# Context attention: weighing by split bf16 products, the maxima's split by ScalarE and GpSimd, and the terms' low halves by GpSimd

## The reference, cut to what matters

```python
# stage 4 (and stage 6 without mask, 8 heads): query 4x512, context 4x154
scores = jnp.einsum('bhqd,bhkd->bhqk', q, k)
scores = jnp.where(mask[:, None, :, :], -1e18, scores)
attn = jax.nn.softmax(scores, axis=-1)
context = jnp.einsum('bhqk,bhkd->bhqd', attn, v)
```

## Time and profile before

| | |
|---|---|
| median of three runs | 1929.69 us (1927.9 to 1934.78) |
| profiled execution, its own time | 1934.83 us |
| its span | 1933.0 us |
| PE busy / DVE / ACT / POOL over the span | 78% / 62% / 41% / 39% |
| mean granted TensorE clock | 0.868 of full speed |
| stage 4, units of the context attention | about 1103 to 1271 us of the span |
| stage 6, units of the context attention | about 1496 to 1607 us of the span |

### The profile page before, as it was taken

The page is one execution under the profiler, slowest core; times in us unless marked ns, Lnnn a source line. Parts: engine busy times, 40 slices in busy tenths (PEclk is TensorE's granted clock), DMA queues, the critical chain, the costliest instruction groups (busy, mean ns, idle before and its releaser), DMA issues.

```text
span 1933.0 us, 32091 instructions
## 1 busy us (share of the span) xinstructions
PE 1515.4 (78%) x11458; PEld 990.6 (51%) x11581; DVE 1205.2 (62%) x2958; ACT 802.1 (41%) x1806; POOL 757.9 (39%) x909
## 2 busy tenths in 40 slices
PE   4899989979998986574268789958976886478877
PEld 2677757766776665452155345523443333334544
DVE  5777667767766655547947657644465465676653
ACT  3677557747765644320035245533212452211111
POOL 3788668858755863510012342000002101143320
PEclk9999989999998997776558799989985697779887
DMA  6223211211211102400000000000000000000000
GB/s 243 76 87 106 76 52 42 55 35 41 53 38 42 51 20 84 150 20 1 0 1 1 11 4 2 1 1 1 1 1 1 1 1 1 1 1 6 1 6 12
DMA packets 35443, 63.94 MB, mean 33 GB/s; under 512 B 7527, under 2 KB 25026, under 8 KB 34131
## 3 DMA queue, kind: packets, MB, share of 16 engines
q1 hardware_dynamic: 33815, 59.77, 10.3%
q0 software_dynamic: 1472, 2.12, 0.3%
HBM read 30.59 MB, written 12.66 MB: 22 GB/s over the span
## 4 chain that ended last, share of the span: by engine, by line
PE 62%; DVE 24%; POOL 5%; issue 5%; ACT 3%; DMA 1%; SPq 0%; DVEq 0%; ACTq 0%; POOLq 0%
PE banks L475 14%; PE banks L694 8%; PE banks L709 6%; PE banks L683 6%; PE banks L1876 4%; DVE xn L421 3%; PE banks L1859 2%; PE banks L450 2%; POOL work L963 2%; PE banks L1785 1%; DVE norm_room L405 1%; PE banks L1826 1%; DVE work L744 1%; PE banks L2565 1%; PE banks L1516 1%
## 5 line engine op out<-in xcount | busy, mean ns | idle before, releaser
L963 POOL TENSOR_TENSOR work<-work 128x512 bf16<-128x512 f32 (+1 forms) x448 | 373.2, 863 | 47.6 <-ACT work L852 44.4
L837 ACT ACTIVATE work<-banks,work 128x666 f32<-128x666 f32 x256 | 209.2, 817 | 198.7 <-DVE work L744 163.3
L415 POOL TENSOR_TENSOR norm_room<-norm_room,minus_half 128x4 f32<-128x4 f32 x48 | 50.2, 1046 | 537.7 <-DVE norm_room L410 537.6
L744 DVE TENSOR_REDUCE work<-banks 128x1 f32<-128x666 f32 x256 | 216.1, 844 | 60.6 <-PE banks L683 60.1
L694 PE MATMUL banks<-const,work 128*128 128x128 f32 (+1 forms) x1536 | 218.5, 279 | 30.0 <-ACT work L852 25.8
L758 DVE COPY work<-banks 128x256 f32<-128x256 f32 x256 | 106.7, 417 | 123.7 <-PE banks L694 123.5
L694 PEld LDWEIGHTS banks<-const,work 128*128 128x128 f32 (+1 forms) x1536 | 156.5, 135 | 51.9 <-ACT work L837 29.3
L683 PE MATMUL banks<-work 128*128 128x154 bf16 (+1 forms) x932 | 172.2, 304 | 7.8 <-DMA work<-work 2.6
L475 PE MATMUL banks<-work,weights_b 128*128 128x512 bf16 (+1 forms) x830 | 157.2, 347 | 12.8 <-DVE work L2200 5.5
L709 PE MATMUL banks<-work 128*64 128x256 bf16 x2304 | 160.7, 284 | 7.5 <-POOL work L963 6.3
L852 ACT ACTIVATE work<-banks 128x512 f32<-128x512 f32 x256 | 151.3, 591 | 10.1 <-PE banks L694 9.8
(11 more groups left out here) (398 smaller groups left out, 3059.7 us busy)
## 6 DMA issues: line engine op xcount, KB each, us to landing
work<-work SPq DMA_DIRECT2D x128, 166.5 KB, 3.0
sorted<-in_pads SPq DMA_DIRECT2D x10, 838.5 KB
weights_b<-in_weights SPq DMA_DIRECT2D x1, 4120.0 KB, 23.4
work<-scratch SPq DMA_DIRECT2D x64, 64.0 KB, 2.0
weights_b<-in_weights SPq DMA_DIRECT2D x1, 2824.0 KB, 9.6
weights_a<-in_weights SPq DMA_DIRECT2D x1, 2056.0 KB, 8.1
weights_a<-in_weights SPq DMA_DIRECT2D x1, 2050.0 KB, 9.4
work<-work SPq DMA_DIRECT2D x32, 64.0 KB, 1.9
```

Of the source, the lines that this page charges most:

```text
L744: ve.tensor_reduce(self.neg_max[i % 4], self.slot[i % 2][:, 0:KEYS0], AX_X, ALU.max, negate=True).then_inc(self.mark("max"))
L837: ac.activation(self.probs[i % 3], self.slot[i % 2][:, 0:KEYS0], ACT.Exp, bias=self.neg_max[i % 4], accum_out=self.sums[u % 4][:, 2 * j + ...
L963: po.tensor_tensor(parts[:, :, :, 0], exact, parts[:, :, :, 1], ALU.subtract).then_inc(self.mark(event, i - 3))
```

## The change

The weighing is done in bf16: with values v and terms t both split as high + low, the product v.t becomes high.high + high.low + low.high (the pairs (1,1), (1,0) and (0,1) of the code, 1 being the upper half; low.low is left out), and the sums need two products, since the ones are exact. So a weighing has 12 + 8 bf16 products of 256 columns in place of 4 + 4 float32 ones. What it needs in addition are the low halves: of the values, once a batch by POOL (`values_low`), and of every term, by POOL, except for two of the 20 a unit in stage 4, which DVE does (`low_by_ve`). The split of the maxima goes from DVE to ACT (high part) and POOL (low part). A chunk is weighed two chunks behind the terms and no longer one, and the last chunk after the "lift" of the next unit; the ring of term tiles grows from 12 to 16. POOL now walks through the sorted list as the others do, so that masks, heads and `query_low` get due times. The rest chunk's mask product in stage 4 is taken over all 128 rows (rows without keys are zeroed once) and no longer over 26.

```diff
-HALF, TERMS = SEQ // 2, 12
+HALF, TERMS = SEQ // 2, 16
...
                 terms += [("term", u, c, g) for g in range(GROUPS)]
-                if c:
-                    terms.append(("weigh", u, c - 1, 0))
-            terms.append(("weigh", u, a.chunks - 1, 0))
+                if c >= 2:
+                    terms.append(("weigh", u, c - 2, 0))
+            terms.append(("weigh", u, a.chunks - 2, 0))
             out += [(u + 1.38 + 0.88 * i / len(terms), *item) for i, item in enumerate(terms)]
-            out += [(u + 2.27 + 0.1 * j, "divide", u, j, 0) for j in range(2)]
-            out.append((u + 2.56, "finish", u, 0, 0))
+            out += [(u + 1.44 + 0.88 * i / len(terms), "low", *item[1:]) for i, item in enumerate(terms) if item[0] == "term"]
+            out.append((u + 2.33, "weigh", u, a.chunks - 1, 0))
+            out += [(u + 2.36 + 0.1 * j, "divide", u, j, 0) for j in range(2)]
+            out.append((u + 2.6, "finish", u, 0, 0))
+        for b in range(1, BATCH):
+            out += [(2 * b - 1.6, "mask", b, 0, 0), (2 * b - 0.8, "query_low", b, 0, 0), (2 * b + 0.3, "mask_t", b, 0, 0)]
+            out += [(2 * b - 1.5 + 0.12 * g, "heads", b, g, 0) for g in range(GROUPS + 1)]
...
+    def low_by_ve(self, a, c, g):
+
+        return a.stage == 4 and c % 2 == 1 and g == 0
...
                 if s == 4:
-                    mask = a.mask_t[b % 2]
-                    if c < a.per_group:
-                        m = pe.matmul(bank, self.cb["eye_b"], mask[:, 0, cols], start=False, stop=True)
-                    else:
-                        m = pe.matmul(bank, self.cb["four_eyes"][0:CTX_REST, :], mask[0:CTX_REST, 1, cols], start=False, stop=True)
+                    mask, rest = a.mask_t[b % 2], c == a.per_group
+                    m = pe.matmul(bank, self.cb["four_eyes" if rest else "eye_b"], mask[:, int(rest), cols], start=False, stop=True)
...
-                pe.wait_ge(*self.at("exp4", s, n))
-                for of_sums in (0, 1):
+                pe.wait_ge(*self.at("term_low", s, n))
+                if self.low_by_ve(a, c, 0):
+                    pe.wait_ge(*self.at("term_low_0", s, n - GROUPS + 1))
+                terms = [self.halves(self.term(a, u, c, g)[3]) for g in range(GROUPS)]
+                values = [self.halves(a.values[b % 2][0:rows_n, c, g, :]) for g in range(GROUPS)]
+                for of_values, of_terms in ((1, 1), (1, 0), (0, 1)):
                     for g in range(GROUPS):
-                        left = a.block[0:rows_n, c, :] if of_sums else a.values[b % 2][0:rows_n, c, g, :]
-                        m = pe.matmul(self.bank_of(5)[WIDE * g:WIDE * (g + 1), of_sums * HALF:(of_sums + 1) * HALF], left,
-                                      self.term(a, u, c, g)[3], start=c == 0 and not of_sums, stop=c == a.chunks - 1, skip_group_check=True)
+                        pe.matmul(self.bank_of(5)[WIDE * g:WIDE * (g + 1), 0:HALF], values[g][:, :, of_values], terms[g][:, :, of_terms],
+                                  start=c == 0 and of_values == of_terms == 1, stop=False, skip_group_check=True)
+                for of_terms in (1, 0):
+                    for g in range(GROUPS):
+                        m = pe.matmul(self.bank_of(5)[WIDE * g:WIDE * (g + 1), HALF:SEQ], self.halves(a.block[0:rows_n, c, :])[:, :, 1],
+                                      terms[g][:, :, of_terms], start=False, stop=c == a.chunks - 1, skip_group_check=True)
...
+            elif what == "negate":
+                ac.wait_ge(*self.at("most", s, 2 * a.steps * (u + 1) - 1))
+                ac.wait_ge(*(self.at("lifted", s, u - 2) if u >= 2 else self.at("clear_shift", s)))
+                ac.activation(a.shift[u % 2][:, :, 0, 0:a.heads], a.most[u % 2], ACT.Copy).then_inc(self.mark("shift_high", s, u))
...
+            for mask in a.mask_t:
+                i = po.memset(mask[:, 1, :], 0.0)
+            po.wait_ge(*self.own("po", i))
             self.mask_t_po(po, a, 0)
-            self.follow_power(po, 3, BATCH - 1)
-        for b in range(1, BATCH):
-            if s == 4:
-                self.mask_po(po, b)
-            self.heads_of(po, a, b)
-            self.query_low(po, a, b)
...
+        for what, u, c, g in self.context_items(a):
+            if what == "negate":
+                out = a.shift[u % 2][:, :, :, 0:a.heads]
+                po.wait_ge(*self.at("shift_high", s, u))
+                po.tensor_tensor(out[:, :, 1, :], a.most[u % 2], out[:, :, 0, :], ALU.subtract).then_inc(self.mark("shift", s, u))
+            elif what == "low" and not self.low_by_ve(a, c, g):
+                n, _, _, whole = self.term(a, u, c, g)
+                po.wait_ge(*self.at("exp4", s, n))
+                po.tensor_tensor(self.halves(whole)[:, :, 0], whole, self.halves(whole)[:, :, 1],
+                                 ALU.subtract).then_inc(self.mark("term_low", s, n))
+            elif what == "values":
+                po.wait_ge(*self.at("values", s, u))
+                for rows, chunks in ((P, slice(0, a.per_group)), (a.rest, slice(a.per_group, a.chunks))):
+                    whole = a.values[u % 2][0:rows, chunks, :, :].rearrange("p c g n -> p (c g n)")
+                    i = po.tensor_tensor(self.halves(whole)[:, :, 0], whole, self.halves(whole)[:, :, 1], ALU.subtract)
+                i.then_inc(self.mark("values_low", s, u))
```

More of the change, by code:

```diff
@@ L1964, in context_ve @@
                                  a.block[0:a.rest, a.per_group:a.chunks, :].to_broadcast([a.rest, GROUPS, WIDE]), ALU.mult).then_inc(self.mark("values", s, u))
[L1965 to L1970 removed]
+            elif what == "low" and self.low_by_ve(a, c, g):
+                n, _, _, whole = self.term(a, u, c, g)
+                ve.wait_ge(*self.at("exp4", s, n))
+                ve.tensor_tensor(self.halves(whole)[:, :, 0], whole, self.halves(whole)[:, :, 1],
+                                 ALU.subtract).then_inc(self.mark("term_low_0", s, n))
             elif what == "divide":
@@ L1984, in context_ve, with heads_of @@
                 self.follow_scale(ve, u, c)
-    def heads_of(self, po, a, b):
-        last = 2 * a.chunks * GROUPS
-        if b >= 3:
-            po.wait_ge(*self.at("termed", a.stage, (b - 2) * last - 1))
-        for g in range(GROUPS):
+    def heads_of(self, po, a, b, g):
+        if b >= 3 and g == 0:
+            po.wait_ge(*self.at("termed", a.stage, (b - 2) * 2 * a.chunks * GROUPS - 1))
+        if g < GROUPS:
             if b in (0, 2):
```

35 lines of the change are left out of this document (19 added, 16 removed).

## The result

The changed kernel takes 1953.07 us (median, 1949.47 to 1955.14) where the kernel before takes 1928.8 us (1927.62 to 1934.78) on the same chip: ratio 1.0122, 95% interval 1.0107 to 1.0137. It is 1.2% slower; 1915 us was forecast, with a range of 1903 to 1933. The profiled execution took 1951.82 us, its span is 1950.0 us, mean clock 0.863. The medians differ by 24.3 us and the two spans by 17.0, because the profiled execution of the kernel before was 6.0 us above its median, and that of the changed kernel 1.3 us under.

The account below looks back on a forecast made before the run. The prediction took PE's time to pace both stages, 152 and 102 us. Stage 4 -10.5, stage 6 -7.9 and clock +4 sum to -14.4, from 1929.7 to 1915 us; range 1903 to 1933.

Parts of the forecast that it names:

- PE's saving: Stages 4 and 6: a weighing falls from 1.00 to 0.68 us; a stage 4 unit loses 2.5 us of PE.
- the wait of 5.97 us: First window of stage 4: PE's wait for `query_low` of batch 1 goes, counted as -6.0 us.
- the new wait for the maxima's split: First window of stage 4: the split stands on POOL behind other tasks, so terms start 3 us later.
- Rivals 1 and 4: 1: PE stays the bound everywhere, 1899 us, chance 0.12; 4: loads of weights show, weighing 1.2 us, 1944 us, chance 0.04.
- POOL can start on the mask while PE still has the last scores and the last weighing, about 2 us: Stage 4, second and fourth windows: this lead shortens POOL's 23.4 us of work to windows of 21.4 us.
- The sixth has POOL at 13.0 against 14.2 of PE: Stage 4, sixth window: PE stays the bound; third, fifth, sixth and seventh windows save 2.5 us each.
- DVE beside POOL: DVE's operations wait some 2 us a unit beside POOL, with 4 to 8 us free: no cost.
- Rival 5: Low halves take 0.9 us because DVE and POOL block each other: +26, 1955 us, chance 0.07.
- rival 2: POOL is dearer, low halves at 0.75 us each: +3, 1933 us, no change, chance 0.18.
- Stage 6, -7.9 forecast: Stage 6: -4.2 in the first three units, -1.0 in most later ones, start +0.3, together -7.9 us.
- clock +4: Stages 4 and 6: PE's new idle time brings stretches of lower clock, costing 4 us.
- Rival 3: The clock falls to 0.7 in all stage 6 windows, 12 us, stage 4 loses 4: 1928 us, no change, chance 0.14.

Follow-up runs that it names:

- e3: The changed kernel without the terms' low halves, products reading the upper half twice, so the output lacks them: 1919.5 us, ratio 0.9948.
- e5: The changed kernel with three of five pieces of each batch's heads (spread keys) due one unit earlier on POOL: ratio 1.0042.
- e4: The changed kernel with DVE's two low halves a unit of stage 4 given to POOL: 1952.5 us, ratio 1.0118.
- e8: The changed kernel with the layer norms' power on POOL placed 0.21 unit later, just ahead of the scaling: ratio 1.0137.
- e6: The changed kernel with 20 idle products a unit added on PE in stage 6, output untouched: 1938.25 us, ratio 1.003.
- e7: The changed kernel with the float32 weighing again and no low halves of terms or values, in both stages: ratio 0.998.
- e14: The changed kernel with chunks 0, 1, 2 of five split in stage 4, three heads pieces a unit earlier, and before's code in stage 6: ratio 0.9924.
- e15: The changed kernel with float32 weighing and no low halves in stage 4, and before's code in stage 6: ratio 0.9913.
- e1b: The changed kernel with the change in stage 4 only and before's context functions in stage 6: 1934.02 us, ratio 0.9994.

## Why the prediction was wrong

**PE's saving: right.** A weighing takes 0.68 us as forecast, the pairs stand 0.11 apart, the wait of 5.97 us is gone, and the first window ends 5.0 us earlier (6.0 forecast; the new wait for the maxima's split, put at 3.0, is 4.2). e3's stage 4 has 2.0 to 2.7 us less in each window at full clock, where 2.0 to 2.5 were forecast. The load of weights does not show, as the earlier trace rows had it and against the rule of the Trainium skill (TensorE: Matmul & The Clock Gate, Part 3, The mechanism) that the prediction quotes; the same section also lets a load go ahead into a background buffer, and which of the two is at work no run tells. Rivals 1 and 4 are out.

**"POOL can start on the mask while PE still has the last scores and the last weighing, about 2 us": the step that failed in stage 4.** The work was reckoned well, 24.0 us from 1136.26 to 1160.29 where 23.4 were forecast, and the lead was there: the mask starts 2.4 us ahead of the window. But the same 2.4 us stand at the window's other end, between POOL's last low half and the next division, and the forecast took the lead off without adding them. There PE's first term of the next unit is behind the last weighing, and that behind POOL's last low half, so POOL has nothing to do. Lead and tail cancel, and the window is as long as the work: 24.0, not 21.4. The two even windows are 2.6 and 2.9 us over the forecast, and PE, which waits in them, now gets spells of half clock (0.89; one runs from 1157.4 to 1164.2, right behind its longest wait, 2.80 us up to 1156.95), and 0.96 in the odd windows, which are 0.9 and 1.1 over. e5 is the test: of 3.6 us moved out of each of these windows, 2.9 and 3.2 came back.

**"The sixth has POOL at 13.0 against 14.2 of PE", -2.5 each: wrong too.** The last three windows are 3.6, 3.5 and 1.5 us over the forecast with neither engine full (14.52 and 12.87 of 17.80). Without low halves they are 14.6, 12.8 and 10.6 (e3), so it is POOL's part in the loop, though not its sum. Taking the larger of two engines' sums is right only if each has work ready while it waits for the other. Which wait of the loop costs how much I can't say in full: DVE's low halves are some 0.8 of the sixth, the power's wait 0.5 of the seventh at most (e4, e8).

**DVE beside POOL, "no cost": too low, and small.** One line of the changed kernel, in the whole span (minimum, median, maximum in ns):

```profile
L1987 DVE TENSOR_TENSOR work<-work x16: 440/493/3924, 1122.9 to 1267.6; 128x256 bf16<-128x256 f32 x16
```

One low half of DVE stood for 3.92 us beside a run of POOL's. POOL's own kept their 0.57 us (six in 3.48 us, the last one's end included). The Trainium skill (GPSIMD Engine Reference, Key points) names this contention, and the trace agrees for DVE. Rival 5, in which this contention decides, needed 0.81 us a low half, and rival 2 needed 0.75. That rival 5's total, 1955 us, is near the measured one is chance.

**Stage 6, -7.9 forecast, 12.8 lost, and "clock +4": the larger miss.** Two steps failed. The first took PE as the bound of the even and the last windows. POOL's part at full clock is at most 2.5 us in each even window (13.3 against 10.8) and 2.8 in the last three (30.6 in e6 at a clock of 1.00, 30.7 in the change at 0.83, against 27.8), 7.8 together. The second is the clock, and its account is a remainder, not a test: 97.2 less 77.4 of the old code is 19.8, which leaves 12.0 for it, while before's own execution had 7.0 of such time (84.4 less 77.4), so 5 are new. Rival 3 was the one with a falling clock, 0.7 in all windows at 12 us; it was 0.82 to 0.85 in the even and last windows and 0.51 and 0.56 in the odd ones. The saving of 7.9 us never came either: e3, without the terms' low halves, takes 86.2 us. And e7 splits the loss another way: 89.5 us without split or low halves, so 5.1 of the 12.8 come with the rest of the change, which I had put at nothing, and 7.7 with the split. What makes the clock fall in the odd windows stays open.

So the miss to the last division is 17.1 us in stage 4 and 20.7 in stage 6, less the 4 allotted: 33.8, and -14.4 + 33.8 is the 19.4 measured between the two profiled executions. The medians are 24.3 us apart; the difference is the 2.4 us that come back behind the last division, and the 7.3 us by which the profiled executions stand closer than the medians. Should before's usual executions have 77.4 us in stage 6, this would be most of those 7.3 us, but no run shows it. Of the whole loss against what PE gives without waiting for low halves, 1.74 points of the ratio (1.0122 less 0.9948) go with the terms' low halves.

## What to carry to other kernels

When work moves from the bound engine to an idle one, don't compare the two sums: walk the in-order lists of both at the hand-over and ask what each has ready while it waits. If the last piece of one unit stands ahead of the first of the next on both engines, a lead at one end of a period is paid back as a wait at the other, and the times add up. Spread the helper's other tasks over the windows with slack before giving it more, and split only as much as fits under the bound engine's window: 8 or 12 low halves a unit of stage 4 did, 18 didn't. And time the parts of a change apart, stage by stage: here all but the split weighing was a gain of 10 us in stage 4, hidden by the part that gave the change its name, and a loss of clock in stage 6 (89.5 us, where the old code behind the same stage 4 takes 77.4).

## What the hardware showed that I had not expected

- The same instructions of stage 6 took 77.4 or 84.4 us (83.2 in e14 and e15) from one kernel to another, with the granted clock of its windows (1.00 in its second to fifth in e1b, a mean of 0.68 over the first three before); executions of one kernel spread by 23 us (e6). A difference of 0.5% in a total says little here without the clock of its windows.
- Time saved on TensorE came back as half clock in e3, whose odd windows in stage 6 have 14.84 us busy of 17.40 at 0.71 where before's has 11.68 of 14.00 at 1.00. But e7, with the float32 products, has 17.28 of 19.70 at 0.65: the rest of the change was enough for it, without that saving.
- One DVE operation with two inputs in SBUF lasted 3.92 us (1235.46 to 1239.38), eight times its median, beside six back-to-back low halves of POOL in 3.48 us, which were not slowed.
